# Attention of two head groups ahead of the expert tiles, router behind the projections, three q/k buffers, a new SBUF layout

## What is computed

```
xn  = layernorm(x)                        # no gain, no shift
qkv = xn @ qkv_w.T + qkv_b                # 16 heads of 16 features
scores = q @ k.T / 4 + slope[h] * (k_pos - q_pos), causal
attn_out = softmax(scores) @ v  ->  @ out_w.T + out_b
# mixture of experts on the same xn
s = sigmoid(xn @ gate_w); selected = top2(s + expert_bias); gates = s[selected] / sum
shared = (silu(xn @ shared_gate_w) * (xn @ shared_up_w)) @ shared_down_w
routed = sum over the 2 selected experts: gate * ((silu(g) * u) @ experts_down[e]),  g, u = split(xn @ experts_gate_up[e])
y = x + attn_out + shared + routed
```

## Time and profile before

| | |
|---|---|
| median of 3 runs | 530.18 us |
| the profiled execution | 529.71 us |
| its span (first to last instruction) | 527.9 us |
| TensorE busy | 464.8 us (88%) |
| VectorE busy | 326.4 us (62%) |
| ACT busy | 246.8 us (47%) |
| POOL busy | 198.3 us (38%) |
| mean granted TensorE clock | 0.952 of 2.4 GHz |
| HBM traffic | 37.27 MB read, 27.13 MB written |

### The profile page before, as it was taken

The page is one execution under the profiler, slowest core; times in us unless marked ns, Lnnn a source line. Parts: engine busy times, 40 slices in busy tenths (PEclk is TensorE's granted clock), DMA queues, the critical chain, the costliest instruction groups (busy, mean ns, idle before and its releaser), DMA issues.

```text
span 527.9 us, 9035 instructions
## 1 busy us (share of the span) xinstructions
PE 464.8 (88%) x3049; PEld 270.7 (51%) x3050; DVE 326.4 (62%) x610; ACT 246.8 (47%) x567; POOL 198.3 (38%) x239
## 2 busy tenths in 40 slices
PE   4596899667858999978989989999999999989998
PEld 4455788445535666754434343444434444322576
DVE  4868985514433656676857767777686777744332
ACT  2610662112212333324747667576676667768300
POOL 3470777699940000008888888500000000000000
PEclk9789799959889999997989999999999999999999
DMA  9898898789999334324113333121220000010022
GB/s 282 191 395 262 280 323 279 267 152 180 191 180 201 119 111 127 121 71 136 42 57 116 98 83 115 48 81 49 60 72 13 3 3 3 1 12 7 3 85 76
DMA packets 65704, 64.60 MB, mean 122 GB/s; under 512 B 21934, under 2 KB 59538, under 8 KB 65634
## 3 DMA queue, kind: packets, MB, share of 16 engines
q1 hardware_dynamic: 51506, 47.85, 30.8%
q0 software_dynamic: 13056, 15.83, 14.1%
q10 hardware_dynamic: 1104, 0.41, 0.3%
HBM read 37.27 MB, written 27.13 MB: 122 GB/s over the span
## 4 chain that ended last, share of the span: by engine, by line
PE 60%; DMA 15%; DVE 9%; POOL 7%; issue 4%; SPq 2%; ACT 2%; POOLq 0%; DVEq 0%
PE ps L1249 11%; PE ps L1235 11%; PE ps L1223 10%; DMA x_in<-sorted_tokens 7%; PE ps L1148 6%; POOL sorted_tokens L543 6%; PE ps L1269 5%; PE ps L1164 4%; DVE mx L971 4%; PE ps L1044 2%; DMA ks<-aux_rows 2%; SPq L455 2%; PE ps L1238 2%; PE ps L1224 2%; DMA qs<-nr 2%
## 5 line engine op out<-in xcount | busy, mean ns | idle before, releaser
L719 ACT ACTIVATE pt<-ps 128x512 f32<-128x512 f32 (+3 forms) x384 | 166.1, 492 | 89.3 <-PE ps L1238 66.2
L971 DVE TENSOR_REDUCE mx<-ps 128x1 f32<-128x384 f32 (+6 forms) x189 | 156.5, 865 | 59.5 <-PE ps L1224 57.9
L1249 PE MATMUL ps<-pt,vg 128*32 128x512 f32 (+3 forms) x768 | 81.2, 498 | 0.0
L576 POOL DMA_INDIRECT yg<-sorted_outputs,slot_i x32 | 32.0, 1000 | 92.0 <-DMA sorted_outputs<-y_out 83.3
L1148 PE MATMUL ps<-w_gu,hx 128*128 x192 | 57.4, 426 | 4.2 <-issue 3.0
L1235 PE MATMUL ps<-qs,ks 111*128 111x512 bf16 (+3 forms) x192 | 56.0, 334 | 5.0 <-DMA qs<-nr 5.0
L1235 PE MATMUL ps<-qk 111*128 111x512 bf16 (+3 forms) x192 | 54.2, 328 | 5.6 <-DMA qk<-nr 4.2
L936 DVE COPY y_out<-ps 128x256 f32<-128x256 f32 x48 | 20.4, 425 | 57.2 <-PE ps L1164 55.1
L1238 PE MATMUL ps<-cbf 128*128 128x128 bf16 x256 | 52.2, 222 | 0.0
L1223 PE MATMUL ps<-qk 108*128 108x512 bf16 (+3 forms) x192 | 50.8, 331 | 0.5 <-DVE mx L971 0.5
L692 ACT ACTIVATE hx<-ps 128x384 f32<-128x384 f32 (+1 forms) x48 | 22.9, 478 | 58.6 <-PE ps L1138 55.9
(11 more groups left out here) (175 smaller groups left out, 736.1 us busy)
## 6 DMA issues: line engine op xcount, KB each, us to landing
sorted_tokens<-y_out SPq DMA_DIRECT2D x12, 512.0 KB, 5.0
qk_parts<-parts SPq DMA_DIRECT2D x16, 384.0 KB, 3.5
x_in<-sorted_tokens SPq DMA_DIRECT2D x48, 128.0 KB, 2.6
sorted_outputs<-y_out SPq DMA_DIRECT2D x48, 128.0 KB, 1.7
w_gu<-e_gu SPq DMA_DIRECT2D x1, 2816.0 KB, 13.1
x_sb<-x SPq DMA_DIRECT2D x4, 512.0 KB, 8.4
w_dn<-e_dn SPq DMA_DIRECT2D x1, 2048.0 KB, 8.4
y<-x_sb SPq DMA_DIRECT2D x16, 128.0 KB, 1.7
```

Source lines behind the costliest of these rows:

```text
L576: g_.indirect_dma_start(out=yg[:, n % 4, :], out_offset=None, in_=ysd, in_offset=bass.IndirectOffsetOnAxis(ap=slot_i[:, k, t:t + 1], axis= ...
L719: sc.activation(pt[:, s % 2, j, lo:CH], bank(n % 3)[:, lo:CH], ACT.Exp).then_inc(s_exp, 1)
L971: last = v.reduce_max(dst, src, axis=AX.X)
L1249: ins = te.matmul(ps[32 * j:32 * j + 32, OUT_BANK * CH + lo:(OUT_BANK + 1) * CH], vg[:, par, kb, j, :], pt[:, s % 2, j, lo:CH], start=kb = ...
```

## The change

The router's jobs come last in `JOBS`, and the q/k jobs come ahead of all v jobs, groups 0 and 1 first. SP loads groups 0 and 1 between the stores of the parts, then stores the rest of the parts and clears the sorted list, and loads group 2 (ahead of the maxima of group 1's end) and the expert weights. The row maxima of group 0 run beside the shared expert as those of any other group. The first pair of groups is attended before the expert tiles, which are now a plain unrolled sequence without maxima between them; POOL's scatter runs meanwhile. SP spreads the sums. NBUF is 3. Tensors that live at different times share regions of SBUF. The copy of the aux rows in HBM is gone, since both sequences read the same rows.

```diff
-NBUF = 4
+NBUF = 3
+COPY_AT = (6, 15, 24)
...
-                + [("b", 0, 0)] + [("o", oc, 0) for oc in range(2)] + [("g", n, 0) for n in range(T // CH)]
-                + [("r", 0, 0)])
-        for n in range(TT // 2):
-            JOBS += [("qk", 2 * n % 4 + k, n // 2) for k in range(2)] + [("v", n, 0)]
+                + [("b", 0, 0)] + [("o", oc, 0) for oc in range(2)])
+        JOBS += [("qk", side * 2 + fc, b * 2 + tc) for b in range(B) for fc in range(2) for side in range(2)
+                 for tc in range(2)]
+        JOBS += [("v", n, 0) for n in range(TT // 2)] + [("g", n, 0) for n in range(T // CH)] + [("r", 0, 0)]
...
+            for i in range(RING):
+                store_parts(i)
+            sp.wait_ge(s_auxst, 4 * DMA)
+            for i in range(4):
+                sp.wait_ge(s_parts[i], DMA)
+            load_group(0)
+            for i in range(RING, RING + 4):
+                store_parts(i)
+            load_group(1)
+            for i in range(RING + 4, NQK):
+                store_parts(i)
+
+            sp.wait_ge(s_zero, 2)
+            xz = xsd.rearrange("(p k) d -> p (k d)", p=P)
+            for n in range(NT // 4):
+                sp.dma_start(xz[:, n * 4 * D:(n + 1) * 4 * D], zeros[:, :, :].rearrange("p k d -> p (k d)")
+                             ).then_inc(s_clear, DMA)
...
+            store_neg(0, 0)
+            sp.wait_ge(s_sh, TT // 2)
+            for i, stored in enumerate(s_parts):
+                sp.wait_ge(stored, DMA * len(range(i, NQK, RING)))
+            load_group(2)
+            sp.dma_start(w_gu[:, :, :, :], e_gu.rearrange("e (c p) f -> p e c f", p=P)).then_inc(s_wgu, DMA)
+            store_neg(1, 1)
+            sp.wait_ge(s_scat, K_TOP * TT * DMA)
+            sp.dma_start(w_dn[:, :, :], e_dn.rearrange("e f d -> f e d")).then_inc(s_wdn, DMA)
+            for k in range(4):
+                load_tile(k)
+            next_group(3)
+            spread_sums(0)
+            store_neg(2, 0)
 
             for k in range(4, 7):
-                next_tile(k, k % 4)
...
+                load_tile(k)
+            for k in range(NT):
+                if k + 7 < NT:
+                    load_tile(k + 7)
+                store_tile(k)
+
+            next_group(4)
+            spread_sums(1)
+            for g in range(2, NG - 1):
+                store_neg(g + 1, (g + 1) % 2)
+                if g + NBUF < NG:
+                    next_group(g + NBUF)
+                spread_sums(g)
...
             for g in range(0, NG, 2):
                 pair(g)
+                if g == 0:
+                    experts()
...
+            shared_gate_up(0)
+            shared_gate_up(1)
+            rank()
+            for c in range(4):
+                if c in (1, 2):
+                    shared_gate_up(c + 1)
+                shared_down(c)
+                if c == 0:
+                    pe.wait_ge(s_free, NJ)
+                    for half in range(2):
+                        pe.wait_ge(s_ld[half][0], LOADS * DMA)
+                for p in range(c * NP // 4, (c + 1) * NP // 4):
+                    max_scores(0, 0, p)
```

More of the change, by code:

```diff
@@ L148, in sem, with region @@
             return ctx.enter_context(nc.semaphore(name))
+        def region(*layouts):
+            tops = []
+            for layout in layouts:
+                with ExitStack() as here:
+                    tops.append([here.enter_context(nc.sbuf_tensor(*t)) for t in layout])
+            sizes = [sum(-(-math.prod(t[1][1:]) * (2 if t[2] == BF16 else 4) // 32) * 32 for t in layout)
+                     for layout in layouts]
+            sb(layouts[0][0][0] + "_region", [P, max(sizes) // 4])
+            return tops
         x_sb = sb("x_sb", [P, TT, D])
@@ L163, in build @@
         gates = sb("gates", [P, K_TOP, TT])
[L164 removed]
+        token = sb("token", [P, 4])
         vg = sb("vg", [P, 2, QT, HG, 32])
[L166 to L224, removed]
[L225 to L237 removed]
@@ L366, in load @@
             dst, order = (q_buf, k_buf)[side][g % NBUF], (Q_PARTS, K_PARTS)[side]
[L367 removed]
+            done = s_ld[half][g % NBUF]
             cols = slice(half * CH, (half + 1) * CH)
@@ L487, in _, with spread_sums, next_group, load_tile @@
-            for g in range(NG):
+            def spread_sums(g):
+                sp.wait_ge(s_ev, g * 2 + 3)
+                sp.dma_start(sums[:, 0, g, :], ot(g)[HD::32, :].rearrange("j (c s) -> j c s", s=HG * S // P)
+                             ).then_inc(s_sums[max(0, g - (NG - 3))], DMA)
+            def next_group(g):
+                sp.wait_ge(s_st, (g - NBUF + 1) * (HG * NS))
+                load_group(g)
+            def load_tile(k):
+                if k >= 4:
+                    sp.wait_ge(s_hxt, k - 3)
+                sp.dma_start(x_in[:, k % 4, :], xsd[k * P:(k + 1) * P, :]).then_inc(s_xin[k % 4], DMA)
@@ L895, in _ @@
             v.tensor_tensor(wsl[:, :, :, :], ws[:, :, :, :], wsh[:, :, :, :], ALU.subtract).then_inc(s_small_l, 1)
-            for n in range(X0, G0):
-                low(n)
-            for n in range(G0, NJ):
+            for n in range(X0, NJ):
                 low(n)
@@ L996, in beside @@
                         maxima(g + dg, q, p)
-            negate(0, 0, first=True)
+            shared_hidden(0)
+            shared_hidden(1)
+            for c in range(4):
+                if c in (1, 2):
+                    shared_hidden(c + 1)
+                for n in range(2):
+                    add_shared(2 * c + n)
+                for p in range(c * NP // 4, (c + 1) * NP // 4):
+                    if p == NP - 1:
+                        negate(0, 0)
+                    else:
+                        maxima(0, 0, p)
             for p in range(EARLY):
@@ L1181, in tile_steps @@
-            def tile_steps(j, first, last):
-                k = j * NTH
-                for u in range(NTH):
-                    tile_step(k + u, u, NTH - u if last else NT, (j * (NTH // 4) + (u + 3) // 4 + 1) * DMA)
-                    for q in range(QT):
-                        if FIRST_AT[q] == u:
-                            first_scores(j, q, j * QT + q, first)
-            pe.wait_ge(s_sha, 2)
-            for k in range(2):
-                tokens_in(k, k, (k + 1) % 2, DMA).then_inc(s_hxt, 1)
```

408 lines of the change are left out of this document (162 added, 246 removed).

## The result

The changed kernel takes **568.7 us** (565.5 to 572.3, four runs), the kernel before on the same chip 530.2 us (529.5 to 531.3). The ratio is 1.073, interval [1.065, 1.080]. Slower was the likelier side of the forecast, but 535 us is 34 us short and the range ended at 544: **the prediction is wrong in size**.

The account below looks back on a forecast made before the run. Bound: TensorE idle in the tiles' first half, where q/k and tile loads compete. Sum: 151.5 to first exponential + 90.8 tiles + 287.4 attention + 3.0 = 532.7, 534.5 with 1.8 around it; median 535 us, range 517 to 544.

Parts of the forecast that it names:

- Attention, "nothing" for the spreading of the sums: Attention: SP's spreading of the sums costs nothing beside exponentials; 287.4 us from 240.5 us to the end remain.
- Group 0, +2.5 us: Attention: group 1's rows land late behind group 2's load and the expert weights; 2.5 us, bounds 0 and 6.
- The ring: Projections: the thirteenth q/k job waits for a slot while SP issues group 0's load for 22.2 us; stall 20 us.
- Router and maxima stage: Front: route and place 17.6 us, up to 104.5; shared expert with group 0's maxima 43 us, then rows 4 us.
- rival (B): Maxima and shared expert: low clock and contention slow gate/up and expose maxima matmuls; 543 us, chance 0.12.
- Tiles: Expert tiles: 47 intervals of 1.75 us (1.70 to 1.93), 82.3 us; with filling and emptying 90.8 us.
- (C): Scatter ahead of the tiles: it is not hidden, ending 27 us later than forecast; chance under 0.02, within B.
- Groups 2 to 6: Attention's later groups: time as before (158.1 us); gathers starting with group 2 and three buffers add nothing.
- Rival (A): Ring: it stalls less, 526 us if the load holds SP 13.2 us, 518 if not at all; chance 0.25.
- The rule beside it: Group loads: DMAs from SP are generally faster than GpSimd's, so at most 13.2 us instead of 22.2; sum 526.
- the 20.8 us of idle time in the first half of the tiles: Kernel before, tile stage: TensorE idles where POOL's q/k loads and tile loads compete; the change can win this time.
- The forecast of +4.8: Whole kernel: the summed 534.5 us against 529.7 us for the profiled execution of the kernel before.

Follow-up runs that it names:

- Experiment 2: Changed kernel with the rows of group 1 stored ahead of the gate/up expert weights; ratio 1.064 [1.059, 1.069] to the kernel before.
- experiment 3: Changed kernel with all sixteen stores of parts ahead of the loads of groups 0 and 1; 557.0 us in the profiled execution, beside 552.4.
- three repairs: Changed kernel: group 6's sums spread by POOL, group 1's rows ahead of expert weights, all parts stored ahead of loads; ratio 1.013, on another chip 0.999 (527.8 us).

## Why the prediction was wrong

- **Attention, "nothing" for the spreading of the sums.** This is the step that failed: 16 us, half of the miss. I counted SP's new DMAs as small ones beside exponentials. The runs show a wait of 3.3 us of TensorE, since the inverted sums of groups 0 to 5 are queued behind the wait for group 6, and then a clock of 0.50 for 31 us. Taking that wait away brings the last group from 76.0 back to 60.1 us. The sum took all from the first group's start to the end as it was.
- **Group 0, +2.5 us.** The mechanism was named, the size was wrong: +9.2 instead (43.5 against 34.3), beyond the bound of 6. I had the rows landing 2.5 us late; in fact their issue, too, was held, for 7.3 us instead of 1.9, and they landed in 6.1 instead of 2.0. Experiment 2 shows that the weights did it.
- **The ring.** Right, and each link as named. The start was 2.6 us late, the queue held 0.9 longer, the landing took 2.1 more: 5.6 us in all, just above the upper bound. Undoing it brings 18 us by the first exponential and 22 by group 1 (experiment 3); the forecast said 20.
- **Router and maxima stage.** Route and place took 17.5 us (17.6 predicted); the stage to the first scores 44.7 (47.0). Of rival (B) only the clock came: it was 0.84 there, and the stage still shorter.
- **Tiles.** The interval is 1.84 us, not 1.75, inside the bounds of 1.70 and 1.93; 47 x 0.09 = 4 us. The scatter was hidden, as said against (C).
- **Groups 2 to 6**, +4.6 us where nothing was forecast. Groups 2 and 3 take 34.2 and 34.0 us instead of 31.3 and 31.8; group 2 has a wait of 3.2 us for its successor's rows, group 3 a mean clock of 0.92. The gathers begin beside these two groups now, and in the kernel before it was groups 0 and 1, beside which they began, that took 34.3 and 34.2. The stretch varies by up to 5 us between runs with and without split loads, so the cause stays open.
- **Rivals.** Rival (A) did not happen. The rule beside it (the Trainium skill, DMA: Bandwidth & Descriptors, section Issuing engine by pattern), that DMAs from SP are generally faster, went against the trace again: 23.1 us of SP for a group, against 13.2 of GpSimd. Most of the gap between my two rows, 22.2 and 13.2 us, hangs on the shape of the loads: with single parts SP needs 17.6 us and GpSimd 14.3.
- **The reading of the kernel before.** I took the 20.8 us of idle time in the first half of the tiles as what the change could win by moving work. An edit of three lines wins as much in place. The share of 1.00 at only 176 GB/s, beside 0.90 at 300 one row above, was the sign: busy engines that move little. The Trainium skill's rule on outer sizes (same page, section Why a DMA increments its semaphore by 16 and not by 1) stood in the forecast, but for SP's queue alone.
- **A slip in the sum's last comparison.** Attention would break even with a start at 146.7 us (240.5 less 90.8 of tiles and 3.0 of additions), not at 145. The forecast of +4.8 doesn't use it.

The gain expected of the change is real in its place, but smaller than what it exposes. On one chip the kernel before with split loads takes 529.0 us, and the change with split loads and all three repairs 541.0. The latter has its tiles at 1.84 instead of 2.12 us, 47 x 0.28 = 13 us. But the maxima of group 0 stand ahead of all attention instead of between the tiles: in that stage of the changed kernel TensorE is busy for 31.7 of 45 us. In the two traces the new front ends with the first exponential at 158.7 us, the old one with the first tile at 122.6: 36 us lost. The tiles, with filling, take 95 us instead of 118: 23 won. The rest differs by 2. That is a reading of two traces; no run moved the maxima alone. The best version of this study is the kernel before with one-part loads.

## What to carry to other kernels

When an instruction moves to another queue, write down what stands behind it there and when it becomes ready, for the last round of the loop too; a wait of 3 us ahead of a long TensorE stretch cost 7 to 16 here. Where a DMA share is high and the GB/s low, look at the shape of the DMAs before moving them: here a split into DMAs of one part was worth 4 to 5%, while no version of the reordering without it beat the kernel before. Undo suspects together as well as singly, since a transfer that is put first delays another: three repairs brought 7 us less than their sum.

## What the hardware showed unexpectedly

- After a pause of about 3 us TensorE's granted clock stayed at 0.50 for up to 31 us with the engine busy in every window. Experiment 2 has it as long. Experiment 3, with the same wait, shows 0.56 and 0.58 in two windows of 4 us, then 1.00, 0.77 and 0.80. What decides the length isn't shown.
- Chips differ: 530 or 552 us for one and the same kernel. On the slower ones, VectorE, ACT or both, and TensorE with them, pause for up to 19 us while GpSimd issues indirect DMAs.
- Six DMAs of one part are issued faster than three of 3, 2 and 1 parts with the same data: 3.7 against 5.4 to 6.7 us on SP. On GpSimd they take longer (3.0 against 2.6 us) and the kernel still gains 24 us.
- Three DMAs of 8 KB behind one of 4 MB took 7.3 us to issue and 6.1 to land, against 1.9 and 2.0 one group earlier.
